# A graph-network kernel on one core: VectorE's half of a dense stage cut in three, with the next group's front between the parts, and ScalarE's exponent ahead of its copies

## The reference

```python
def _demo_layer(h, src, dst, deg_pos, inv_deg, Wg, Wl, Ws, b):
    g = h @ Wg
    neigh_mean = jax.ops.segment_sum(h[dst], src, num_segments=h.shape[0]) * inv_deg[:, None]
    extra = neigh_mean @ Wl + h @ Ws
    out = g + deg_pos[:, None] * extra + b
    return jax.nn.elu(out)
...
h = _demo_layer(x, ...Wg1, Wl1, Ws1, b1)
h = _demo_layer(h, ...Wg2, Wl2, Ws2, b2)
return _demo_layer(h, ...Wgo, Wlo, Wso, bo)
...
x = _layernorm(x + _L0_gnn_ref(...), axis=-1)
x = _layernorm(x + _L1_gnn_ref(...), axis=-1)
```

## Time and profile before

| | |
|---|---|
| median of the runs | 9617.37 us |
| profiled execution, its own time | 9606.42 us |
| its span | 9604.6 us |
| mean granted TensorE clock over the span | 0.771 of full speed |
| three layers, first start of a back half to the start of the thirteenth | 97.21, 84.38 and 153.49 us |
| 14 groups in each layer | 42 in all |

### The profile page before, as it was taken

The page is one execution under the profiler, slowest core; times in us unless marked ns, Lnnn a source line. Parts: engine busy times, 40 slices in busy tenths (PEclk is TensorE's granted clock), DMA queues, the critical chain, the costliest instruction groups (busy, mean ns, idle before and its releaser), DMA issues.

```text
span 9604.6 us, 193424 instructions
## 1 busy us (share of the span) xinstructions
PE 6594.0 (69%) x46642; PEld 5845.8 (61%) x46642; DVE 5951.8 (62%) x16064; ACT 3698.9 (39%) x9003; POOL 4757.6 (50%) x4833
## 2 busy tenths in 40 slices
PE   7899999940079998655566675657664566656667
PEld 6788889940079997555445665446653455545556
DVE  8899997520076665554775445854448756546657
ACT  0011110000068887776593112951126954431111
POOL 0027777777734444776005662036640056647760
PEclk5555555555589999777799997999987988878876
DMA  9988887666589998878499994998974999987770
GB/s 383 391 279 199 199 198 179 157 157 158 149 273 326 332 331 283 239 237 215 146 396 315 302 301 106 394 342 294 302 197 158 393 353 352 353 237 218 213 188 14
DMA packets 1665463, 2463.57 MB, mean 256 GB/s; under 512 B 985413, under 2 KB 1057081, under 8 KB 1665385
## 3 DMA queue, kind: packets, MB, share of 16 engines
q1 hardware_dynamic: 1325672, 1499.58, 46.0%
q0 software_dynamic: 292608, 911.36, 32.7%
q10 hardware_dynamic: 47104, 51.75, 2.5%
HBM read 1435.51 MB, written 1022.63 MB: 256 GB/s over the span
## 4 chain that ended last, share of the span: by engine, by line
DMA 24%; PE 22%; issue 16%; DVE 14%; POOL 13%; ACT 7%; ACTq 2%; DVEq 2%; SPq 1%; POOLq 0%
PE ps L830 10%; DMA frows<-by_src 10%; POOL by_src L645 9%; DMA oht_g<-ones 4%; DMA ring<-gathered,gidx 4%; PE ps L823 3%; PE ps L905 3%; DMA rows<-by_src,gidx 2%; DMA gathered<-ring 2%; ACT ring L1204 2%; DVE mask L1484 2%; POOL ring L720 2%; POOL ring L700 2%; DVE ohj L1393 2%; DVE prod L1471 2%
## 5 line engine op out<-in xcount | busy, mean ns | idle before, releaser
L720 POOL DMA_INDIRECT ring<-gathered,gidx x2176 | 2130.3, 979 | 2634.6 <-DMA gathered<-ring 1584.4
L645 POOL DMA_INDIRECT by_src<-prow,ppos x1562 | 1524.2, 976 | 1108.7 <-DMA ppos<-pos 636.2
L823 PE MATMUL ps<-hring,oht_g 128*128 128x192 bf16 x8704 | 1031.7, 257 | 659.5 <-DMA oht_g<-oht 255.4
L1561 DVE TENSOR_REDUCE red<-ps 128x256 f32<-128x768 f32 x680 | 649.4, 955 | 1108.3 <-PE ps L905 934.9
L830 PE MATMUL ps<-frows,hring 128*128 128x193 f32 x4352 | 954.1, 368 | 533.4 <-DMA frows<-by_src 335.8
L823 PEld LDWEIGHTS ps<-hring,oht_g 128*128 128x128 fp8e4 x8704 | 713.6, 101 | 905.7 <-issue 867.7
L830 PEld LDWEIGHTS ps<-frows,hring 128*128 128x128 f32 x4352 | 799.1, 213 | 616.6 <-issue 412.7
L905 PE MATMUL ps<-ring,oht_g 128*128 128x192 bf16 x7616 | 921.0, 270 | 257.7 <-DMA ring<-gathered,gidx 122.5
L1639 DVE CAST ring<-ps 128x384 bf16<-128x384 f32 x1632 | 838.8, 553 | 254.8 <-PE ps L823 220.0
L788 PE MATMUL ps<-snap,oht_e 98*128 98x98 f32 x3130 | 956.0, 445 | 0.0
L905 PEld LDWEIGHTS ps<-ring,oht_g 128*128 128x128 fp8e4 (+1 forms) x7616 | 735.8, 109 | 350.8 <-issue 312.8
(11 more groups left out here) (240 smaller groups left out, 12635.4 us busy)
## 6 DMA issues: line engine op xcount, KB each, us to landing
gathered<-ring SPq DMA_DIRECT2D x408, 768.0 KB, 5.8
by_src<-zeros SPq DMA_DIRECT2D x34, 6272.0 KB, 46.6
frows<-by_src SPq DMA_DIRECT2D x544, 392.0 KB
oht_g<-oht SPq DMA_DIRECT2D x544, 256.0 KB, 5.9
gathered<-got SPq DMA_DIRECT2D x136, 776.0 KB, 6.2
oht_g<-ones SPq DMA_DIRECT2D x408, 256.0 KB
prow<-in_edge_attr_n SPq DMA_DIRECT2D x284, 352.0 KB
gathered<-frows SPq DMA_DIRECT2D x136, 384.0 KB
```

Of the source, the lines that this page charges most:

```text
L645: pool.indirect_dma_start(out=table, out_offset=bass.IndirectOffsetOnAxis(ap=ppos[:, s, j:j + 1], axis=0), in_=prow[:, s, j, :], in_offset ...
L720: pool.indirect_dma_start(out=ring[:, c, :], out_offset=None, in_=rows_of, in_offset=offsets(g, c % 4)).then_inc(q.got[c], 16)
L823: mm = pe.matmul(ps[:, bank + k // 2, k % 2 * HW:(k % 2 + 1) * HW], eight(one_hots)[:, k * P:(k + 1) * P], parts, start=True, stop=True, s ...
L1561: return dve.tensor_reduce(red[:, u, :, 0:D], sums_of(bank)[:, :, 0:HW].rearrange("p b (a d) -> p b d a", d=D), AX.X, ALU.add)
```

## The change

VectorE's back half becomes three functions. `split(i)` is the part up to the maximum; `joined(i)` is the part from the wait for the exponent up to the value (in the third layer up to the variance); `parts(i)` is the rest (in the third layer from the wait for the square root on). The front is cut as well: `front` keeps the operations up to `acc * inv`, and `rest` has the two additions, the last of which raises `q.cat`. For a group i VectorE now does split(i), front(i + 2), then rest(i + 2) and joined(i) (in the third layer joined(i) and then rest(i + 2)), and parts(i). On ScalarE the exponent and the zeroing stand ahead of the copies of transposed(i + 2), and the square root just ahead of them. TensorE's stream and the DMA queue's stay as they are; no operation is added or taken away.

```diff
             def layer(q):
-                def group(i, u):
+                def exponent(i, u):
                     ts = bass.ds(i * NT, NT)
                     act.wait_ge(q.neg, i + (q.c0 + 1))
                     act.activation(nbs[u], nbs[u], ACT.Exp).then_inc(q.exp, 1)
                     act.activation(acc[:, ts, :], iota_part[:, 0:1].unsqueeze(2).to_broadcast([P, NT, D]), ACT.Copy,
                                    scale=0.0)
-                    if q is node3:
-                        root(q, i, nms[u])
+
+                def group(i, u):
+                    ts = bass.ds(i * NT, NT)
...
                 with act.Fori(0, NGROUPS // 2 - 1) as half:
                     for u in range(2):
+                        exponent(2 * half + u, u)
                         act.wait_ge(q.mm, 2 * half + (q.c0 + u + 1))
+                        if q is node3:
+                            root(q, 2 * half + u, nms[u])
                         transposed(q, 2 * half + (q.c0 + u + 3), u, u)
                         group(2 * half + u, u)
...
                     dve.tensor_tensor(cat[:, :, D:P], acc[:, ts, :], spread_over(inv[:, ts]), ALU.mult)
+
+                def rest(i, u):
+                    cat = cats[u]
+                    step = Steps(q.front, i, per_front)
+                    step.n = per_front - 1
+                    ts = bass.ds(i * NT, NT)
                     step(dve.tensor_tensor(cat[:, :, 0:D], hb[:, ts, 0:D], hb[:, ts, D:2 * D], ALU.add))
                     dve.tensor_tensor(cat[:, :, 0:D], cat[:, :, 0:D], hb[:, ts, 2 * D:3 * D], ALU.add).then_inc(q.cat, 1)
...
+                def back(i, u, half, ahead):
+                    split(i, u, half)
+                    dve.wait_ge(q.tr, i + (q.c0 + 1))
+                    front(ahead, u)
+                    if normed:
+                        joined(i, u, half)
+                        rest(ahead, u)
+                    else:
+                        rest(ahead, u)
+                        joined(i, u, half)
+                    parts(i, u)
 
                 for u in range(2):
                     front(u, u)
+                    rest(u, u)
                 for u in range(2):
-                    dve.wait_ge(q.tr, q.c0 + u + 1)
-                    front(2 + u, u)
-                    back(u, u, 0)
+                    back(u, u, 0, 2 + u)
                 with dve.Fori(1, NGROUPS // 2 - 1) as half:
                     for u in range(2):
-                        dve.wait_ge(q.tr, 2 * half + (q.c0 + u + 1))
-                        front(2 * half + (u + 2), u)
-                        back(2 * half + u, u, half)
+                        back(2 * half + u, u, half, 2 * half + (u + 2))
```

More of the change, by code:

```diff
@@ L1301, in layer @@
                     for u in range(2):
+                        exponent(2 * half + u, u)
                         act.wait_ge(q.mm, 2 * half + (q.c0 + u + 1))
+                        if q is node3:
+                            root(q, 2 * half + u, nms[u])
                         transposed(q, 2 * half + (q.c0 + u + 3), u, u)
                         group(2 * half + u, u)
-                group(NGROUPS - 2, 0)
-                group(NGROUPS - 1, 1)
+                for u in range(2):
+                    exponent(NGROUPS - 2 + u, u)
+                    if q is node3:
+                        root(q, NGROUPS - 2 + u, nms[u])
+                    group(NGROUPS - 2 + u, u)
             def last(q):
@@ L1755, in upper_half, with spread_out @@
                 return high(ap)[:, :, 1::2]
-            def layernorm(q, step, i, na, nb, nm):
+            def spread_out(q, step, na, nb, nm):
                 step(dve.tensor_reduce(nm[:, :, 0], na, AX.X, ALU.add))
@@ L1763, in layernorm, with scaled @@
                 dve.tensor_scalar(nm[:, :, 1], nm[:, :, 1], 1.0 / D, EPS, ALU.mult, ALU.add).then_inc(q.var, 1)
+            def scaled(q, step, i, nm):
                 dve.wait_ge(q.std, i + 1)
@@ L1786, in front, with split @@
                     assert step.n == per_front, step.n
-                def back(i, u, half, final=False):
+                def split(i, u, half, final=False):
                     na, nb, nm, ps = nas[u], nbs[u], nms[u], ps_o[u]
                     step = Steps(q.v, i, per_back)
-                    ts = bass.ds(i * NT, NT)
                     dve.wait_ge(q.mm, i + (q.c0 + 1))
@@ L1800, in back, with joined @@
                     step(dve.tensor_scalar(na, na, 0.0, -1.0, ALU.max, ALU.add))
+                def joined(i, u, half, final=False):
+                    na, nb, nm = nas[u], nbs[u], nms[u]
+                    step = Steps(q.v, i, per_back)
+                    step.n = 4
                     dve.wait_ge(q.exp, i + (q.c0 + 1))
@@ L1813, in back @@
                     dve.tensor_tensor(hb[:, ts, 2 * D:3 * D], nb, upper_half(nb), ALU.subtract).then_inc(q.done, 1)
-                    assert step.n == per_back, (step.n, per_back)
+                def back(i, u, half, ahead):
+                    split(i, u, half)
+                    dve.wait_ge(q.tr, i + (q.c0 + 1))
+                    front(ahead, u)
+                    if normed:
+                        joined(i, u, half)
[4 more added lines that the diff above has]
+                    parts(i, u)
                 for u in range(2):
                     front(u, u)
+                    rest(u, u)
                 for u in range(2):
-                    dve.wait_ge(q.tr, q.c0 + u + 1)
-                    front(2 + u, u)
-                    back(u, u, 0)
+                    back(u, u, 0, 2 + u)
                 with dve.Fori(1, NGROUPS // 2 - 1) as half:
                     for u in range(2):
-                        dve.wait_ge(q.tr, 2 * half + (q.c0 + u + 1))
-                        front(2 * half + (u + 2), u)
-                        back(2 * half + u, u, half)
+                        back(2 * half + u, u, half, 2 * half + (u + 2))
                 if normed:
                     dve.memset(xress[1][:, NT - 1, :], 0.0).then_inc(s_hpad, 1)
-                back(NGROUPS - 2, 0, NGROUPS // 2 - 1, True)
-                back(NGROUPS - 1, 1, NGROUPS // 2 - 1, True)
+                for u in range(2):
+                    split(NGROUPS - 2 + u, u, NGROUPS // 2 - 1, True)
+                    joined(NGROUPS - 2 + u, u, NGROUPS // 2 - 1, True)
+                    parts(NGROUPS - 2 + u, u)
                 dve.wait_ge(q.done, q.c0 + NGROUPS)
@@ L1872, in finish @@
                     step(dve.tensor_tensor(na, na, hs, ALU.add))
-                    layernorm(q, step, i, na, nb, nm)
+                    spread_out(q, step, na, nb, nm)
+                    scaled(q, step, i, nm)
                     assert step.n == 10, step.n
```

10 lines of the change are left out of this document (8 added, 2 removed).

## The result

The changed kernel takes **9679.92 us** (median of 4 runs, 9665.16 to 9693.75) against 9619.19 us (4 runs, 9608.22 to 9624.15) for the kernel before, measured beside it: a ratio of 1.0065, 95% interval 1.0049 to 1.0081. It is slower by 61 us, 0.65%, as forecast (9683, range 9653 to 9706).

What follows compares the result with a forecast made beforehand. VectorE was taken as the bound, with a 34.1 us hole in 42 groups. Waiting for TensorE's product adds 66 us to 9606.4, making 9672; the runs' median lies 10.95 us higher, so 9683 us, range 9653 to 9706.

Steps and rivals of the forecast that it cites:

- The mechanism: Three dense layers: VectorE would wait 2.4 to 2.7 us a group for TensorE's product, in a loop; 91%.
- What goes: VectorE's waits for the exponent, 16.8 and 17.3 us, and the third layer's square root wait, 0.28 us a group, would go.
- rival C: Product ready in time, VectorE the bound with its holes closed: 27 us less, 9590 us; 2%.
- Tile ready: Time from L1810's start until TensorE's tile is ready: 5.83, 4.76 and 9.20 us in the three layers.
- hand-over from split to front: VectorE's step between the two parts, put at 0.05 us.
- L: Time from the front's end to the product's end, taken as 4.50 us, bounds 3.96 and 4.80.
- The start behind the product: VectorE's delay in starting after TensorE's product, estimated at 0.04 us.
- The sum: Twelve groups in each of three layers: +27.2, +27.2 and +11.4 us, in all +66 us.
- Costed at nothing: ScalarE's copies, the third layer's exponent table load (1.283 us) and the residual's DMAs would add no time.
- D: A wait costed at nothing shows, such as the third layer's table load: +84 us and more, 9701 and up; 2%.
- B: TensorE's clock stays at 2.4 GHz with L at 2.56 us: 4 us less, 9613 us, no change; 5%.
- The break-even of L = 2.67 us: The L at which twelve new groups of each layer would take the former 335.08 us.

Runs made afterwards that it cites:

- e2: The changed kernel with TensorE doing product(i + 1) ahead of turn(i + 2); 9595.8 us, ratio 0.9970 to the kernel before.
- e1: The changed kernel with VectorE back in its old order, ScalarE's new order kept; 9600.0 us, ratio 0.9972 to the kernel before.
- e7: The changed kernel with the ten groups of VectorE's loop written out, waits on constants; 11209.7 us, ratio 1.0054 to the kernel before.
- e8: The kernel of e2 with the ten groups of VectorE's loop written out; 11117.8 us, ratio 0.9967 to the kernel before.
- e6: The changed kernel with 48, 36 and 82 extra TensorE transposes a group in the three layers; 11118.1 us, ratio 1.0015 to the kernel before.
- e4: The changed kernel with 30 extra TensorE transposes a group, 60 in the third layer; 9670.8 us, ratio 1.0047 to the kernel before.

## Why the prediction was right

**The mechanism.** It named the loop split(i), front(i + 2), turn(i + 2), product(i + 1), split(i + 1), with TensorE's unchanged order as its cause. e2 turns that order alone and takes out 91.7 us. This is shown. e1, with VectorE's old order, has no such wait either.

**What goes.** The exponent's wait went (34.1 to 2.8 us) and the wait ahead of the reciprocal L1774, for the square root, went from 7.9 to 4.5 us (the second network's share of it stays). What is left of the exponent's wait lies in the last two groups of each layer, which have no front to stand in it. As rival C costed it, closing all holes would bring 27 us; with the order mended in e2 it is 21.8 us.

**Tile ready**, predicted 5.83, 4.76 and 9.20 us after L1810. In the group shown above it is 6.09 us. The other two layers:

```profile
5987.42 0.63 DVE L1810 TENSOR_TENSOR oht_g<-ps,layers 128x448 f32<-128x448 f32 x1 [2.94 <-PE ps L977]
5991.80 0.62 DVE L1800 TENSOR_TENSOR ring<-ring,node 128x448 f32<-128x448 f32 x1
5994.03 3.19 PE L977 MATMUL ps<-layers,ring 128*128 128x128 f32 x14
5997.35 0.62 DVE L1810 TENSOR_TENSOR oht_g<-ps,layers 128x448 f32<-128x448 f32 x1 [2.94 <-PE ps L977]
...
7367.41 0.62 DVE L1810 TENSOR_TENSOR oht_g<-ps,layers 128x448 f32<-128x448 f32 x1 [2.04 <-PE ps L977]
7376.11 0.62 DVE L1800 TENSOR_TENSOR ring<-ring,node 128x448 f32<-128x448 f32 x1
7378.34 2.57 PE L977 MATMUL ps<-layers,ring 128*128 128x128 f32 x14
7380.51 1.28 ACT L1289 ACT_TABLE_LOAD   x1
7381.03 0.62 DVE L1810 TENSOR_TENSOR oht_g<-ps,layers 128x448 f32<-128x448 f32 x1 [2.08 <-PE ps L977]
```

They give 5.00 and 9.32 us. The first two groups of each layer, ahead of the loop, have it sooner, at 5.38, 4.53 and 8.76 us. Over all twelve the means are 5.98, 4.93 and 9.28 us, together 0.40 us over the 19.79 predicted, 4.8 us in twelve groups. The mis-sized term is the hand-over from split to front, put at 0.05 us: in the loop L1788 idles 0.28 us for L1815. Written out, in e7 and e8, this idle time is gone.

**L**, predicted 4.50 us, with 3.96 and 4.80 as bounds. Its means over the twelve groups are 4.36, 4.62 and 4.29 us, together 0.24 under the prediction, 2.8 us less in twelve groups; single groups go from 3.94 to 4.80. The start behind the product is 0.12 us in most groups of the loop and not 0.04, which adds 2.1 us. In the second layer most groups are 9.93 us, with L at 4.80, all of it at 1.2 GHz. That the means come so near 4.50 is in part luck: the transposes are at 1.2 GHz in every group, but the product takes 2.3 to 3.2 us by where in it the clock rises, if it does, and that differs from group to group and from kernel to kernel. In e7, with the same steps in the same order, the means are 4.76, 4.53 and 4.77 us. And the bounds came from eight groups of layer 1 alone: in layer 2 of the kernel before, one group has transposes of 0.99 us, behind 2.4 us of idle time, and L at 2.61 us. After the change TensorE idles 4.6 us or more before each front, and no group does that.

**The sum.** Predicted +27.2, +27.2 and +11.4 us; measured +27.7, +31.5 and +10.7. The total of +69.9 against +65.8 is the errors above, 4.8 less 2.8 plus 2.1 us. The idle time ahead of L1810 is 103 us, where "some 95" were named; 14.1 us of it stand ahead of the first group of a layer (5.6 us before), and the rest is 89 us. The wait is a little shorter than forecast and VectorE's own work, with its chained steps, a little longer. The medians differ by 61 us, 9 less than the stretches; the interval of the ratio, 47 to 78 us, holds both. So the 3 us between 9683 and 9679.92 are partly luck, since a sum that was 4 us too low met a measured difference that was 9 us under the stretches'.

**Costed at nothing.** The exponent's table load is hidden: in the rows above it ends at 7381.79, and the exponent of that group starts at 7383.56, when the minimum is there (its idle time is put down to L1814). D did not occur.

**The rivals.** B did not occur by itself. Forced in e6, its group in the first layer's loop is 8.84 us in the rows shown (8.74 every other time) and not 8.43: 0.26 more for the tile, 0.08 for the start and 0.06 for L. The three stretches are 351.4 us where rival B said 331.1, the first two groups of each layer included, which the fill doesn't reach. The break-even of L = 2.67 us was set too high. With the measured mean tiles (20.20 us in all) and starts (0.30 in all) it is (27.92 - 20.20 - 0.30) / 3 = 2.47 us, under the L of e6's loop, 2.6. C's condition, the order of the two steps, is what e2 made true.

## What to carry to other kernels

When a producer's step is moved behind its consumer's first part to fill a wait, follow the loop it closes through every other engine's stream: if the step that the mover needs next stands behind the step that the move delays, the two streams run one after the other. Turn both orders together, as in e2, or leave the first alone, as in e1, which alone brought 16.4 of e2's 21.8 us. The 3.5 us by which the product was early in the earlier trace rows were no time to spare: they were there because a whole back half and a front covered L, the 4 to 4.8 us from the front's end to the product's end.

## What the runs showed of the hardware

**Work that makes TensorE faster.** At 30 transposes of fill a group, with 3.0 us of idle time behind them, most of layer 1's next transposes ran at 1.2 GHz (1.76 us); at 48, with 0.96 us, they ran at 2.4 GHz (0.98 us), and the layer, 124.91 us in the changed kernel, took 107.73 us. The Trainium skill ("TensorE: Matmul & The Clock Gate", Part 4: PE-mode transpose) says that the full clock doesn't engage for transposes, which don't count as work on TensorE in the same way. The trace of e6 differs: its fill is transposes alone (fp32, 128 x 128), the products and transposes beside it are those of the changed kernel, and the granted clock of e6's stretches is 0.93 and 0.94 against 0.63.

**In the loop, chained VectorE operations are slower.** Where the code is written out and the waits are on constants, it is 0.42 us from the start of a 0.39 us operation to the next; in the loop, with waits on register values, 0.67 us. Over a group of the first layer it is 0.83 us of 7.99. No idle time for the loading of the written-out code shows: behind the first group of a layer VectorE has no gap of over 0.1 us in layers 1 and 2 of e8. Whether the register's value or the loop's own instructions cost it was not tried apart.

**The granted clock of an early stage says little.** Windows of the first 1000 us, the kernel before and e4, with the same instructions in it:

```profile
0.00:1000.00 1000.00, 896.30 (x4941) 781.18 (x4942) 912.34 (x2569) 96.17 (x169) 280.32 (x289) 0.51 0.92 309
```
```profile
0.00:1000.00 1000.00, 896.10 (x4939) 781.42 (x4940) 910.86 (x2568) 96.04 (x169) 282.16 (x292) 1.00 0.93 309
```

TensorE's busy time is the same at 0.51 and at 1.00 (896.30 and 896.10 us). The 1.00 isn't a measured level: e4's trace holds no record of the clock before 2692 us, and the profile then counts it as full; in that of the kernel before the records start at 16 us, and from 19 to 2695 us they say 0.5. So the mean clock of a whole span (0.772 for the changed kernel, 0.916 for e4) does not tell two runs apart; the stretch in question has to be read by itself.
